# Moving a reload, reordering the engines' lists and letting TensorE add the residual of one feature tile in a graph-network kernel

## Chip, cores, metric

One NeuronCore of a Trainium2 chip (trn2). The metric is the device time in microseconds, the median of some runs; lower is better. The program has one launch and all data is in HBM at the start.

## What is computed

The input x has 1250 nodes with 512 features, and 20000 edges (src, dst) sorted by dst. Cut to what matters:

```
h    = relu(layernorm(x))                        # 1250 x 512
xn   = batchnorm(h) * g1 + b1
agg  = segment_sum(xn[src], dst) / max(deg, 1)
conv = relu(agg @ W_conv + b_conv)
attn = performer_attention(h[first 256 positions], Wq, Wk, Wv, proj) @ Wo
out  = x + batchnorm(conv + attn + h) * g2 + b2  # per feature, over the 1250 nodes
```

The attention has 8 heads of 64 and 256 random features; only 256 positions take part, and nodes behind them get the last one's result.

## The kernel before

The program is written out by hand, one list of instructions for each engine; semaphores join them. The eight PSUM banks go round in a fixed order (`order`, `order_end`); `pe_open` waits until the last user of a bank has been read, `landed(eng, name)` waits until TensorE has filled the bank of that name, `stored(eng, name)` until the bank has been read. `link` makes VectorE wait for its own last instruction.

**Front.** Ten node tiles of x are loaded into `xs`, normalised (VectorE statistics, ScalarE `ln_tile`), turned by TensorE and stored feature-major in `hT` by ScalarE (`store_hT`). In VectorE's list come then `edge_values` (the edge list's arithmetic), `weight_sizes` (L1100, waits for W_conv), `constants` (L1086 to L1095), `edge_columns` (L1105, L1106, then a wait until ScalarE has read the bank), the batchnorm statistics `bn_piece(0..2)` (L1040), `bn_mean`, `column_scales`, `bn_scale` and the first `one_hots` (L1054). ScalarE's `edge_columns` (L394, L395) waits for `flag_ready`, which VectorE gives at L1106. TensorE does the attention's projections, then `count()` (L621, a group of 10 one-hot products that counts edges), then `values(0, 0)` and `values(0, 1)` (L630).

**Middle.** 25 groups of edges go round: VectorE `one_hots`, TensorE `count`, ScalarE `store` (L387) into the adjacency `A16`; a count waits until the store two groups before is done. Between them stand the projection of the nodes, `project(i, half)` (L676), which reads `xnT`, made by ScalarE in three parts, `normal_xT(0..2)` (L457), and which ScalarE `high_part` (L497) and VectorE `low_part` (L1193) split into two f16 parts `gh`, `gl`; and the attention. `xnT` lies in the same memory as `xs`, so x must be loaded again for the last sum: SyncE's list has that reload (L306) behind `landed(sp, "G", 9)`, the last projection. `q_feat(7)` is ScalarE's (L479).

**Branch.** Behind the last `attn_T(1)` (L711) TensorE reads `flag` and branches over a block (`uncovered_edges`) that handles edge lists which the fast counting can't cover; with these inputs the block is skipped. Behind it stand `heads_out` (L719, 16 matmuls of 128x128 by 128x256 f32, each of them two records in the trace) and then the edge sums `aggregate(f, c)` (L936), for four feature tiles f and three chunks c of nodes.

**End.** For each feature tile VectorE makes y (`y(f, c)`, L1331, L1336) and its statistics (L1338), `moments` (L1342, L1344) and `scale` (six dependent small steps, L997 to L1000, L1350, L1351), with a square root by ScalarE (L581) between. ScalarE applies scale and shift (L584), TensorE turns the tile back (`transpose_z`, L954), VectorE adds x in place in `xs` (`finish`, L1361), and SyncE and ScalarE issue the stores (L334, L338, L588, L590). Ahead of the last feature tile's transposes stand `LATE` = 14 matmuls whose result nobody reads (L945).

Of the kernel before, what the change touches and what calls it, by code (L numbers as in the profile page):

```python
# [5 lines left out]
ALU = mybir.AluOpType  # L6
# [8 lines left out]
P = 128  # L15
# [27 lines left out]
LATE = 14  # L43
# [11 lines left out]
def gnn_kernel(nc, x, src, dst, g1, b1, g2, b2, w_conv, b_conv, w_q, w_k, w_v, w_o, proj, out):  # L55
    with ExitStack() as ctx:
# [168 lines left out]
        def read(*name):  # L225
            return bank_read[uses[name][0]]
# [77 lines left out]
        def _(sp):  # L304
# [22 lines left out]
            landed(sp, "G", NT - 1)  # L327
# [45 lines left out]
        def _(act):  # L373
# [17 lines left out]
            def edge_columns():  # L391
                acc = landed(act, "cols")
                act.wait_ge(flag_ready, 1)
                act.activation(bcol[:, :, :], acc[:, 0:NW].unsqueeze(2).to_broadcast([P, NW, 2]), ACT.Copy)  # L394
                act.activation(vcol[:, :, :], acc[:, NW:2 * NW].unsqueeze(2).to_broadcast([P, NW, 2]), ACT.Copy  # L395
                               ).then_inc(read("cols"), 1)
# [149 lines left out]
            normal_xT(2)  # L546
            k_exps(1, 1)
            store()
            q_feat(7)
# [3 lines left out]
            store()  # L553
            high_part(6)
            store()
# [9 lines left out]
            attn_copy(0)  # L565
            high_part(9)
# [9 lines left out]
            for c, (c0, cn) in enumerate(CHUNKS):  # L576
                acc = landed(act, "rdeg", c)
                act.activation(rdeg[:, c0:c0 + cn], acc[:, 0:cn], ACT.Copy).then_inc(read("rdeg", c), 1)  # L578
            for f in range(FT):
# [3 lines left out]
                for a, b in ((0, 512), (512, 1024), (1024, N)) if f < FT - 1 else ((0, 512), (1024, N)):  # L583
                    act.activation(yT[:, f, a:b], yT[:, f, a:b], ACT.Identity,  # L584
                                   bias=t2[:, f:f + 1], scale=s2[:, f:f + 1]).then_inc(z_act, 1)
# [8 lines left out]
        def _(pe):  # L594
# [239 lines left out]
            count()  # L834
            pe.wait_ge(wv_in, 16)
            values(0, 0)
            values(0, 1)
# [101 lines left out]

            def transpose_z(f):  # L940
                for j in range(3):
                    acc = pe_open(pe, "zT", f, j)
                    if (f, j) == (FT - 1, 0):
                        for k in range(LATE):
                            nc.tensor.matmul(acc[:, :], cone[:, :], A16[:, 0, 0:512], start=True, stop=True)  # L945
                    if f < FT - 1:
                        pe.wait_ge(z_act, 3 * f + j + 1)
                    elif j == 1:
                        pe.wait_ge(z_dve, 1)
                    else:  # L950
                        pe.wait_ge(z_act, 3 * f + j // 2 + 1)
                    for i in range(4 * j, min(4 * j + 4, NT)):
                        o = (i - 4 * j) * P
                        last = nc.tensor.transpose(acc[:, o:o + P], yT[:, f, i * P:(i + 1) * P], ident[:, :])  # L954
                    last.then_inc(full("zT", f, j), 1)
# [26 lines left out]
            transpose_z(FT - 2)  # L982
# [4 lines left out]
        def _(dve):  # L987
# [115 lines left out]
            def edge_columns():  # L1103
                acc = landed(dve, "cols")
                link(V.tensor_scalar(fl[0:1, 1:2], acc[0:1, 2 * NW:2 * NW + 1], float(NW * P - E), None, ALU.is_equal))  # L1105
                V.tensor_copy(flag[:, :], fl[0:1, 1:2]).then_inc(flag_ready, 1)  # L1106
                stored(dve, "cols")

# [122 lines left out]
            bn_scale()  # L1231
            one_hots()
# [44 lines left out]
            one_hots()  # L1277
            k_feat(1)
# [32 lines left out]
            def last_phase(slow):  # L1311
# [28 lines left out]
                def moments(f):  # L1340
                    c = slice(f, f + 1)
                    V.bn_aggr(mv2[:, f, :], st2[:, f, :, :].rearrange("p c s -> p (c s)")).then_inc(bn2_var, 1)  # L1342
                    dve.wait_ge(bn2_var, f + 1)
                    V.tensor_scalar(bw2[:, 3, c], mv2[:, f, 0:1], -1.0, None, ALU.mult)  # L1344

                def scale(f):
# [3 lines left out]
                    link(V.tensor_tensor(s2[:, c], bw2[:, 1, c], vec[:, 4 * V_G2 + f:4 * V_G2 + f + 1], ALU.mult))  # L1350
                    V.scalar_tensor_tensor(out=t2[:, c], in0=s2[:, c], scalar=bw2[:, 3, c],  # L1351
                                           in1=vec[:, 4 * V_B2 + f:4 * V_B2 + f + 1], op0=ALU.mult, op1=ALU.add).then_inc(st2_ready, 1)
# [25 lines left out]
                finish(f - 1, 0)  # L1378
# [4 lines left out]
                finish(f - 1, 1)  # L1383
                finish(f - 1, 2)
# [81 lines left out]
```

## Time and profile before

| | us |
|---|---|
| median of 3 runs | 198.77 (198.75 to 200.66) |
| the profiled execution | 199.06 |
| its span, first to last instruction | 197.1 |
| TensorE busy in the span | 172.4 (87%) |
| VectorE, ScalarE busy | 130.9 (66%), 89.4 (45%) |
| mean granted TensorE clock | 0.964 of full speed |

The profiled execution is 1.96 us longer than its span; that part lies outside of the instructions. A share of busy time is a mean over stages with different limits.

### The profile page before, as it was taken

To read this page: it belongs to the slowest core of one execution; us is meant where nothing else is said; L and a number is where in the kernel's file an instruction comes from. 1 tells how busy PE (TensorE), PEld (TensorE's weight loads), DVE (VectorE), ACT (ScalarE), POOL (GpSimd) and SP (SyncE) were. 2 spreads that over 40 slices of the span, in tenths; PEclk is the share of its full clock that TensorE was granted. 3 is DMA by queue.
4 is the path that set the end of the run, shared out by engine and by line. 5 is a ranking of instruction groups with operands and counts; after the bars stand their busy time and mean duration, and the time that the engine had idled before them with its cause. 6 is when DMAs were issued, how large, how long until landed. Compare 5 with 4: busy or idle time off the path is not lost.

```text
span 197.1 us, 2982 instructions
## 1 busy us (share of the span) xinstructions
PE 172.4 (87%) x1115; PEld 115.7 (59%) x1116; DVE 130.9 (66%) x311; ACT 89.4 (45%) x159; POOL 7.6 (4%) x22
## 2 busy tenths in 40 slices
PE   0589999799999999979999995089999999999980
PEld 0568797644476546536777674068549465474740
DVE  3678879997465766987737846920203989497591
ACT  3339946285961779994433316001725040404030
POOL 5180000000000000000000000000000000000000
PEclk9999999969999999999999999658999999999999
DMA  5988910000330000000000006900000004022027
GB/s 185 377 246 245 384 37 0 0 0 5 84 145 0 3 0 0 0 5 0 0 3 0 3 0 191 328 7 0 0 0 3 0 0 130 3 62 69 0 61 200
DMA packets 11883, 13.69 MB, mean 69 GB/s; under 512 B 1458, under 2 KB 6748, under 8 KB 11868
## 3 DMA queue, kind: packets, MB, share of 16 engines
q1 hardware_dynamic: 10476, 12.13, 18.9%
q10 hardware_dynamic: 1072, 1.10, 1.7%
q0 software_dynamic: 320, 0.26, 0.7%
q8 instruction: 10, 0.16, 0.3%
q14 instruction: 5, 0.04, 0.1%
HBM read 10.92 MB, written 2.56 MB: 68 GB/s over the span
## 4 chain that ended last, share of the span: by engine, by line
PE 60%; DVE 13%; DMA 9%; ACT 8%; issue 6%; SPq 2%; ACTq 0%; DVEq 0%
PE bank L936 21%; PE bank L676 13%; PE bank L719 5%; DMA xs<-in_x 5%; PE bank L630 4%; DMA wc<-in_L_gnn_W_conv 4%; PE bank L700 4%; PE bank L690 4%; PE bank L621 3%; DVE st L1040 3%; PE bank L653 2%; SPq L306 2%; ACT r L492 2%; PE bank L954 1%; ACT r L387 1%
## 5 line engine op out<-in xcount | busy, mean ns | idle before, releaser
L676 PE MATMUL bank<-wc,xs 128*128 128x512 f32 (+1 forms) x80 | 38.6, 609 | 0.1
L936 PE MATMUL bank<-r,gl 128*128 128x512 f16 (+1 forms) x120 | 38.2, 338 | 0.0
L936 PE MATMUL bank<-r,gh 128*128 128x512 f16 (+1 forms) x120 | 38.1, 339 | 0.0
L1054 DVE TENSOR_TENSOR ohb<-iota,bcol 128x1280 f16<-128x1280 f16 x25 | 20.5, 819 | 4.9 <-PE bank L621 4.8
L387 ACT ACTIVATE r<-bank 128x500 f16<-128x500 f32 x25 | 18.7, 767 | 5.1 <-PE bank L621 5.0
L676 PEld LDWEIGHTS bank<-wc,xs 128*128 128x128 f32 (+1 forms) x80 | 13.6, 187 | 10.8 <-issue 10.8
L936 PEld LDWEIGHTS bank<-r,gl 128*128 128x128 f16 x120 | 11.7, 97 | 9.2
L936 PEld LDWEIGHTS bank<-r,gh 128*128 128x128 f16 x120 | 11.6, 97 | 9.1
L609 PE MATMUL bank<-hT,r 128*128 128x256 f32 x64 | 16.2, 412 | 0.7 <-issue 0.7
L719 PE MATMUL bank<-qe,wvo 128*128 128x256 f32 x32 | 10.1, 491 | 7.1 <-issue 7.1
L1331 DVE SCALAR_TENSOR_TENSOR r<-bank,cinv,r 128x512 f32<-128x512 f32 (+1 forms) x12 | 7.8, 646 | 12.0 <-ACT r L578 6.8
L621 PEld LDWEIGHTS bank<-ohv,ohb 128*128 128x128 f16 x250 | 9.8, 98 | 9.9 <-issue 7.2
L609 PEld LDWEIGHTS bank<-hT,r 128*128 128x128 f32 x64 | 13.0, 208 | 3.1 <-ACT hT L378 1.1
L719 PEld LDWEIGHTS bank<-qe,wvo 128*128 128x128 f32 x32 | 8.1, 256 | 9.0 <-issue 7.3
L581 ACT ACTIVATE bw<-mv,epst 128x1 f32<-128x1 f32 x4 | 1.2, 295 | 25.4 <-DVE mv L1342 25.4
L621 PE MATMUL bank<-ohv,ohb 128*128 128x50 f16 x250 | 10.6, 186 | 2.3 <-DVE ohv L1054 1.3
L1193 DVE SCALAR_TENSOR_TENSOR gl<-bank,gh 128x512 f16<-128x512 f32 (+1 forms) x10 | 6.9, 690 | 7.9 <-ACT gh L497 7.9
L497 ACT ACTIVATE gh<-bank 128x512 f16<-128x512 f32 (+1 forms) x10 | 6.0, 600 | 12.1 <-PE bank L676 12.1
L1054 DVE TENSOR_TENSOR ohv<-iota,vcol 128x500 f16<-128x500 f16 x25 | 10.3, 412 | 0.0
L584 ACT ACTIVATE r<-r,t,s 128x512 f32<-128x512 f32 (+1 forms) x11 | 7.2, 717 | 5.4 <-DVE t L1351 5.4
L630 PE MATMUL bank<-wvo,hT 128*128 128x512 f32 x16 | 9.0, 706 | 0.0
L457 ACT ACTIVATE xs<-hT,t,s 128x384 f32<-128x384 f32 (+2 forms) x12 | 7.8, 734 | 2.6 <-DVE t L1130 2.6
(167 smaller groups left out, 264.9 us busy)
## 6 DMA issues: line engine op xcount, KB each, us to landing
xs<-in_x SPq DMA_DIRECT2D x15, 256.0 KB, 5.0
out<-xs SPq DMA_DIRECT2D x7, 256.0 KB
r<-in_L_gnn_Wq SPq DMA_DIRECT2D x1, 1024.0 KB, 8.3
r<-in_L_gnn_Wk SPq DMA_DIRECT2D x1, 1024.0 KB, 6.2
wc<-in_L_gnn_W_conv SPq DMA_DIRECT2D x1, 1024.0 KB, 8.5
wvo<-in_L_gnn_Wv SPq DMA_DIRECT2D x1, 1024.0 KB, 11.2
wvo<-in_L_gnn_Wo SPq DMA_DIRECT2D x1, 1024.0 KB, 5.2
xs<-in_x ACTq DMA_DIRECT2D x3, 256.0 KB, 4.1
```

The costliest lines, as they stand in the source:

```text
L387: act.activation(A16[:, :, p * GW * W:(p + 1) * GW * W].rearrange("p a (q d) -> p q a d", q=GW), bank[p % 2][:, 0:GW * NT * W].rearrange(" ...
L457: act.activation(xnT[:, f, a:b], hT[:, f, a:b], ACT.Identity, bias=t1[:, f:f + 1], scale=s1[:, f:f + 1]).then_inc(xn_ready, 1)
L609: last = nc.tensor.matmul(acc[:, t * NA:(t + 1) * NA], w[:, f, c:c + P], hT[:, f, 0:NA], start=(f == 0), stop=(f == FT - 1))
L621: last = nc.tensor.matmul(bank[p % 2][:, q * NT * W:(q + 1) * NT * W], ohb[:, s, :], ohv[:, s, :], start=True, stop=True)
L630: last = nc.tensor.matmul(acc[:, :], hT[:, f, t * P:(t + 1) * P], wvo[:, f, :], start=(f == 0), stop=(f == FT - 1))
L676: last = nc.tensor.matmul(acc[0:n, :], xnT[:, f, i * P:i * P + n], wc[:, f, :], start=(f == 0), stop=(f == FT - 1))
L690: last = nc.tensor.matmul(acc[:, j * (DH + 1):(j + 1) * (DH + 1)], kf[:, t, h, m * P:(m + 1) * P], v1[:, t, h, :], start=(t == 0), stop=(t ...
L700: last = nc.tensor.matmul(acc[:, j * (DH + 1):(j + 1) * (DH + 1)], qfT[:, m, h, t * P:(t + 1) * P], kv[:, m, h, :], start=(m == 0), stop=( ...
L719: last = nc.tensor.matmul(acc[:, t * NA:(t + 1) * NA], wvo[:, c, o:o + P], attnT[:, c, :], start=(c == 0), stop=(c == FT - 1))
L936: last = nc.tensor.matmul(acc[:, 0:cn], gg[0:n, s, f * P:(f + 1) * P], A16[0:n, s, c0:c0 + cn], start=(s == 0 and gg is gh), stop=(s == NT ...
L1054: last = V.tensor_tensor(oh[:, s0:s0 + n, :].rearrange("p s (m t) -> p s m t", t=2), iota16[:, 0:size].rearrange("p (m t) -> p m t", t=2). ...
L1331: V.scalar_tensor_tensor(out=yT[:, f, c0:c0 + cn], in0=sums, scalar=cinv[:, f:f + 1], in1=rdeg[:, c0:c0 + cn], op0=ALU.mult, op1=ALU.mult) ...
```

## The change

- SyncE's reload of x waits for the first edge sum (`landed(sp, "agg", 0, 0)`) in place of the last projection.
- ScalarE's `edge_columns` no longer waits for VectorE's flag; it copies the one number that VectorE needs (`fl`) itself. VectorE's part goes behind `bn_scale`, and `bn_piece(0)` goes ahead of `weight_sizes`.
- TensorE's first `count()` goes behind `values(0, 0)`.
- In ScalarE's list `normal_xT(2)` goes from ahead of `k_exps(1, 1)` to behind `high_part(5)` and its two stores, and one `store()` goes ahead of `high_part(9)`; `q_feat(7)` goes to VectorE.
- Feature tile 2 (the third) is turned by matmuls with the identity that add x's tile in PSUM (`turn_with_residual`); ScalarE copies two of its three banks to `xs`, VectorE one, in place of VectorE's three `finish`. The 14 unread matmuls go.
- `scale(f)` has four dependent steps, not six; one short step goes to `moments`.
- ScalarE normalises nodes 0 to 511 of the last tile in two halves, and TensorE waits for each.

```diff
-            landed(sp, "G", NT - 1)
+            landed(sp, "agg", 0, 0)
             for i in range(NT):
                 load_x(i)
...
             def edge_columns():
                 acc = landed(act, "cols")
-                act.wait_ge(flag_ready, 1)
                 act.activation(bcol[:, :, :], acc[:, 0:NW]...)
...
+                act.activation(fl[0:1, 1:2], acc[0:1, 2 * NW:2 * NW + 1], ACT.Copy).then_inc(read("cols"), 1)
...
+            k_exps(1, 1)
+            store()
+            high_part(5)
+            store()
+            store()
             normal_xT(2)
-            k_exps(1, 1)
-            store()
-            q_feat(7)
-            store()
-            high_part(5)
-            store()
-            store()
             high_part(6)
...
+            def copy_turned(f, j):
+                a, b = 4 * j, min(4 * j + 4, NT)
+                acc = landed(act, "zT", f, j)
+                act.activation(xs[:, a:b, f * P:(f + 1) * P], acc[:, 0:(b - a) * P]..., ACT.Copy).then_inc(read("zT", f, j), 1)
+
             for f in range(FT):
+                if f == FT - 1:
+                    copy_turned(f - 1, 0)
                 act.wait_ge(bn2_var, f + 1)
                 act.activation(bw2[:, 0, f:f + 1], mv2[:, f, 1:2], ACT.Sqrt, bias=epst[:, 0:1]).then_inc(bn2_std, 1)
+                if f == FT - 1:
+                    copy_turned(f - 1, 1)
                 act.wait_ge(st2_ready, f + 1)
-                for a, b in (...) if f < FT - 1 else ((0, 512), (1024, N)):
+                for a, b in (...) if f < FT - 1 else ((0, 256), (256, 512), (1024, N)):
...
             features("uk", kT, 1)
-            count()
             pe.wait_ge(wv_in, 16)
             values(0, 0)
+            count()
             values(0, 1)
...
+            def turn_with_residual(f):
+                for j in range(3):
+                    acc = pe_open(pe, "zT", f, j)
+                    pe.wait_ge(z_act, 3 * f + j + 1)
+                    tiles = range(4 * j, min(4 * j + 4, NT))
+                    for i in tiles:
+                        pe.wait_ge(x_in[i], 32)
+                    for i in tiles:
+                        n, o = rows_of(i), (i - 4 * j) * P
+                        nc.tensor.matmul(acc[:, o:o + P], yT[:, f, i * P:(i + 1) * P], ident[:, :], start=True, stop=False)
+                        last = nc.tensor.matmul(acc[0:n, o:o + P], ident[0:n, 0:n], xs[0:n, i, f * P:(f + 1) * P],
+                                                start=False, stop=True)
+                    last.then_inc(full("zT", f, j), 1)
...
-            transpose_z(FT - 2)
+            turn_with_residual(FT - 2)
             transpose_z(FT - 1)
...
             edge_values()
+            bn_piece(0)
             weight_sizes()
             constants()
-            edge_columns()
-            bn_piece(0)
             bn_piece(1)
             link(bn_piece(2))
             bn_mean()
             column_scales()
             bn_scale()
+            edge_columns()
             one_hots()
...
-                    rstd(mv2[:, f, 1:2], bw2[:, 0, c], bw2[:, 1, c], bw2[:, 2, c])
-                    link(V.tensor_tensor(s2[:, c], bw2[:, 1, c], vec[...], ALU.mult))
+                    link(V.reciprocal(bw2[:, 1, c], bw2[:, 0, c]))
+                    V.tensor_tensor(s2[:, c], bw2[:, 1, c], vec[...], ALU.mult)
+                    link(V.scalar_tensor_tensor(out=bw2[:, 0, c], in0=bw2[:, 1, c], scalar=bw2[:, 2, c], in1=bw2[:, 1, c], ...))
+                    link(V.scalar_tensor_tensor(out=s2[:, c], in0=bw2[:, 0, c], scalar=1.5, in1=s2[:, c], ...))
...
                 moments(f)
-                finish(f - 1, 0)
                 scale(f)
...
-                finish(f - 1, 1)
-                finish(f - 1, 2)
+                acc = landed(dve, "zT", f - 1, 2)
+                V.tensor_copy(xs[:, 8:NT, (f - 1) * P:f * P], ...)
```

## Rows read from the trace of the kernel before

Timeline rows are: start, length, engine, line, operation, out<-in, shape, count, and in brackets the idle time before with what ended it. SPq is SyncE's queue. In the rows of stretches (A:B) stand the stretch's length, then busy time of PE, PEld, DVE, ACT and POOL with counts, then the granted TensorE clock, the DMA engines' mean busy share and GB/s. "issue" is time in which an engine waited for nothing that the profile shows.

**Rows 1.** The page: granted clock in 40 slices; the instruction queue of section 3

```profile
PEclk9999999969999999999999999658999999999999
...
q8 instruction: 10, 0.16, 0.3%
```

**Rows 2.** The chain that ended last: start, length, what

```profile
46.44 1.80 PE bank L630 x4
...
121.94 0.61 ACT qe L467
122.54 6.49 issue
129.04 10.06 PE bank L719 x32
```

**Rows 3.** Timeline around the branch: SyncE's queue, the reload of x

```profile
118.60 4.68 SPq L306 DMA_DIRECT2D xs<-in_x  x10
```

**Rows 4.** Stretches around the branch, and one in the edge sums

```profile
121.90:124.60 2.70, 0.00 (x0) 0.00 (x0) 2.49 (x5) 0.60 (x1) 0.00 (x0) 1.00 0.92 296
124.60:127.90 3.30, 0.00 (x0) 0.00 (x0) 3.09 (x5) 0.00 (x0) 0.00 (x0) 0.52 0.94 346
127.90:129.00 1.10, 0.00 (x0) 0.00 (x0) 1.03 (x3) 0.00 (x0) 0.00 (x0) 0.50 0.06 22
...
129.00:134.80 5.80, 5.76 (x14) 4.63 (x15) 0.33 (x2) 0.00 (x0) 0.00 (x0) 0.50 0.01 3
...
148.90:149.30 0.40, 0.40 (x6) 0.40 (x6) 0.00 (x0) 0.38 (x1) 0.00 (x0) 1.00 0.19 41
```

**Rows 5.** Timeline of VectorE, front

```profile
23.58 2.50 DVE L1100 SCALAR_TENSOR_TENSOR gh<-wc 128x512 bf16<-128x512 f32 x4 [0.30 <-DMA wc<-in_L_gnn_W_conv]
...
28.93 6.02 DVE L1040 BATCH_NORM_STATS2 st<-hT 128x6 f32<-128x512 f32 x12 [1.20 <-ACT vcol L395]
...
38.28 0.82 DVE L1054 TENSOR_TENSOR ohb<-iota,bcol 128x1280 f16<-128x1280 f16 x1
```

**Rows 6.** Timeline of ScalarE, front

```profile
21.91 1.06 ACT L378 ACTIVATE hT<-bank 128x512 f32<-128x512 f32 x2
...
27.83 0.59 ACT L394 ACTIVATE bcol<-bank 128x500 f16<-128x500 f32 x1 [2.75 <-DVE flag L1106]
...
29.95 1.94 ACT L378 ACTIVATE hT<-bank 128x512 f32<-128x512 f32 x4
```

**Rows 7.** Timeline of TensorE, front

```profile
39.49 0.60 PE L621 MATMUL bank<-ohv,ohb 128*128 128x50 f16 x10 [1.28 <-DVE ohv L1054]
...
44.94 1.13 PE L653 MATMUL bank<-pT,qT 64*128 64x256 f32 x8
```

**Rows 8.** A stretch of the front, TensorE's clock in it

```profile
39.40:42.60 3.20, 3.11 (x13) 1.58 (x14) 3.17 (x7) 3.17 (x7) 0.00 (x0) 0.50 0.00 0
```

**Rows 9.** Timeline of the middle: waits of VectorE and TensorE, ScalarE's third part of xnT

```profile
61.32 0.17 DVE L1135 COPY diag<-bank 128x16 f32<-128x16 f32 x1 [2.23 <-PE bank L644]
...
83.22 2.40 ACT L457 ACTIVATE xs<-hT,t,s 128x354 f32<-128x354 f32 x4
...
88.01 0.41 PE L621 MATMUL bank<-ohv,ohb 128*128 128x50 f16 x10 [1.07 <-ACT r L387]
```

**Rows 10.** Timeline of VectorE: the first sums with the reloaded x

```profile
163.03 1.60 DVE L1361 TENSOR_TENSOR xs<-bank,xs 128x512 f32<-128x512 f32 x3
```

**Rows 11.** Groups by line and shape, 100 to 197 us: 10 matmuls f32

```profile
L971 PE MATMUL bank<-ident,dcol 128*128 128x128 f32 x20 | 2.4, 275 | 0.0
```

**Rows 12.** Timeline of the end, all engines

```profile
187.02 3.19 PE L945 MATMUL bank<-r,cone 128*128 128x512 f16 x14
...
188.10 0.68 DVE L1361 TENSOR_TENSOR xs<-bank,xs 128x512 f32<-128x512 f32 x1
...
189.92 1.28 ACT L584 ACTIVATE r<-r,t,s 128x512 f32<-128x512 f32 x2 [1.59 <-DVE t L1351]
...
192.54 0.38 SPq L334 DMA_DIRECT2D out<-xs  x1
```

More of the change, by code:

```diff
@@ L42 @@
 SLOW_LINKS = 8
-LATE = 14
 EP, EJ = 125, E // 125
@@ L545, in _ @@
             store()
-            normal_xT(2)
             k_exps(1, 1)
-            store()
-            q_feat(7)
             store()
@@ L553, in _ @@
             store()
+            normal_xT(2)
             high_part(6)
+            store()
             store()
@@ L578, in _ @@
                 act.activation(rdeg[:, c0:c0 + cn], acc[:, 0:cn], ACT.Copy).then_inc(read("rdeg", c), 1)
+            def copy_turned(f, j):
+                a, b = 4 * j, min(4 * j + 4, NT)
+                acc = landed(act, "zT", f, j)
+                act.activation(xs[:, a:b, f * P:(f + 1) * P], acc[:, 0:(b - a) * P].rearrange("p (t n) -> p t n", t=b - a),
+                               ACT.Copy).then_inc(read("zT", f, j), 1)
             for f in range(FT):
+                if f == FT - 1:
+                    copy_turned(f - 1, 0)
                 act.wait_ge(bn2_var, f + 1)
                 act.activation(bw2[:, 0, f:f + 1], mv2[:, f, 1:2], ACT.Sqrt, bias=epst[:, 0:1]).then_inc(bn2_std, 1)
+                if f == FT - 1:
+                    copy_turned(f - 1, 1)
                 act.wait_ge(st2_ready, f + 1)
-                for a, b in ((0, 512), (512, 1024), (1024, N)) if f < FT - 1 else ((0, 512), (1024, N)):
+                for a, b in ((0, 512), (512, 1024), (1024, N)) if f < FT - 1 else ((0, 256), (256, 512), (1024, N)):
                     act.activation(yT[:, f, a:b], yT[:, f, a:b], ACT.Identity,
@@ L949, in transpose_z @@
                         pe.wait_ge(z_dve, 1)
-                    else:
-                        pe.wait_ge(z_act, 3 * f + j // 2 + 1)
+                    elif j == 2:
+                        pe.wait_ge(z_act, 3 * f + 3)
                     for i in range(4 * j, min(4 * j + 4, NT)):
+                        if f == FT - 1 and i in (0, 2):
+                            pe.wait_ge(z_act, 3 * f + i // 2 + 1)
                         o = (i - 4 * j) * P
@@ L1277, in _ @@
             one_hots()
+            q_feat(7)
             k_feat(1)
@@ L1344, in moments @@
                     V.tensor_scalar(bw2[:, 3, c], mv2[:, f, 0:1], -1.0, None, ALU.mult)
+                    V.tensor_scalar(bw2[:, 2, c], mv2[:, f, 1:2], EPS, -0.5, ALU.add, ALU.mult)
                 def scale(f):
@@ L1348, in scale @@
                     dve.wait_ge(bn2_std, f + 1)
-                    rstd(mv2[:, f, 1:2], bw2[:, 0, c], bw2[:, 1, c], bw2[:, 2, c])
-                    link(V.tensor_tensor(s2[:, c], bw2[:, 1, c], vec[:, 4 * V_G2 + f:4 * V_G2 + f + 1], ALU.mult))
+                    link(V.reciprocal(bw2[:, 1, c], bw2[:, 0, c]))
+                    V.tensor_tensor(s2[:, c], bw2[:, 1, c], vec[:, 4 * V_G2 + f:4 * V_G2 + f + 1], ALU.mult)
+                    link(V.scalar_tensor_tensor(out=bw2[:, 0, c], in0=bw2[:, 1, c], scalar=bw2[:, 2, c], in1=bw2[:, 1, c],
+                                                op0=ALU.mult, op1=ALU.mult))
+                    link(V.scalar_tensor_tensor(out=s2[:, c], in0=bw2[:, 0, c], scalar=1.5, in1=s2[:, c],
+                                                op0=ALU.add, op1=ALU.mult))
                     V.scalar_tensor_tensor(out=t2[:, c], in0=s2[:, c], scalar=bw2[:, 3, c],
```

12 lines of the change are left out of this document (4 added, 8 removed).

## The prediction

> **What bounds the kernel now.** I read the granted clock and the queue table of the page first, then the chain that ended last, then the timelines of the engines around each edited step. TensorE is busy for 172.4 of 197.1 us, so the time is its work plus its holes plus what a halved clock costs. The page shows the clock below full at two places, in slice 9 and slices 26 to 28 of 40 [rows 1]; both lie at edits. The large one: the last product ahead of the branch is turned and copied by 122.54, then nothing happens on the chain for 6.49 us, and only at 129.04 does `heads_out` start and take 10.06 us [rows 2]. The reload of x is issued from 118.60 on in ten DMAs [rows 3]; the DMA engines are 92 and 94% busy until 127.90, then one sixteenth of them works for 1.1 us at 22 GB/s (24 KB, a page of instructions of 16 KB and a remainder, or so I read it; the instruction queue moved 10 packets in 0.16 MB, 16 KB each [rows 1]), and then TensorE goes on [rows 4]. My reading: the taken branch needs instructions that must come by DMA, and they come behind x. The clock falls in this hole and stays at 1.2 GHz (0.50) to 134.8, 5.8 us of work [rows 4].
>
> The small one: TensorE waits 1.28 us for the first one-hots, then works 3.1 us at 0.50 [rows 7, 8]. A third hole of 1.07 us lies at 88.01, ended by a store of ScalarE [rows 9]. At the end, the chain leaves TensorE: statistics, scale, normalise, turn, add, store.
>
> **Front, part by part.** VectorE now has 0.30 us of waiting for W_conv and 1.20 us for ScalarE's reading of the columns [rows 5]. `bn_piece(0)` needs node tiles 0 to 3, stored by 22.97 [rows 6], so it starts at 23.3 with no wait. Four 512-column statistics, at 6.02 us for eight of 512 and four of 226 columns, are 2.5 us: to 25.8. `weight_sizes` 2.5 us to 28.3, `constants` 1.4 us to 29.7. ScalarE no longer stands for 2.75 us at the flag [rows 6]; its two column copies and the small one fall into that wait, and its tile stores, which began at 29.95, begin some 0.7 us earlier, when TensorE's key product permits. So tiles 6 and 7 are stored by 30.2, `bn_piece(1)` runs to 32.7, `bn_piece(2)` to 33.9, where before statistics ended at 34.95 [rows 5]. The moved flag step costs 0.2 us ahead of the one-hots. Net about 1.0 us: the one-hots begin at 37.4 and not 38.28, and end at 38.5.
>
> TensorE itself was free at 39.49 - 1.28 = 38.21 [rows 7]. With `values(0, 0)` first it needs no one-hots then: 1.80 us (two matmuls at full clock, the first row of [rows 2]) to 40.0, the count 0.25 us, `values(0, 1)` 1.80 us, so 42.05 against 44.94: 2.9 us, if the clock holds. If the clock falls at 39.3 and rises at 42.6 as now [rows 8], 1.1 us of work is done before, 1.65 in the slow stretch, and the remaining 1.1 ends at 43.7: 1.25 us. I take 2.9, since the hole is gone and dense 512-column work stands in it, bounds 1.2 and 2.9. VectorE and ScalarE are only 1.0 ahead there, yet VectorE stands 2.23 us for TensorE's diagonal at 61.32 [rows 9], and ScalarE then waits for VectorE, so they catch up.
>
> **Middle.** The wait of 1.07 us at 88.01 is for ScalarE's store behind `normal_xT(2)` and `k_exps(1, 1)` [rows 9]. With the 2.3 us of `normal_xT(2)` moved behind, that store comes 2.2 us earlier: the hole closes, 1.05 us. Followed on in before's times, `normal_xT(2)` then runs from 88.8 to 91.0, and `project(7, 0)`, its first reader, comes at 95.0; `q_feat(7)` on VectorE costs it 0.6 us in the 0.9 us in which it waited for ScalarE's exponentials, and the key features are ready at 88.1 for 89.0. Those covers are 4 us and 0.9 us wide; if the second were gone, it would cost up to 0.6. The store ahead of `high_part(9)` fits in a pause of ScalarE: nothing.
>
> **Branch.** The reload now starts after the first edge sum, so nothing but the fetch is in the DMA queues at the branch. No row shows a fetch alone from the branch on. Bounds: `heads_out` can't start before 122.54 [rows 2], a gain of 6.5; and if the queue was not the cause, 0. Nearest row: the 1.1 us of transfer behind the reload [rows 4]. With the branch at about 121.5 and as long again for its way as for its transfer, 2.2 to 2.5 us, TensorE starts at 124.0. Gain 5.0. **Clock:** the fall came 2.7 us after TensorE stood still, at 124.6 [rows 4]; 2.1 us is a shorter hole, but 1.28 us was enough in the front. I expect it to fall and to rise sooner, since dense work then follows at once: 3.3 us slow as in the front [rows 8] and not 5.8, so 1.65 lost in place of 2.9. Gain 1.25, bounds 0 and 2.9.
>
> The Trainium skill (Runtime: NRT & Kernel Launch, section "Instruction fetch mechanics") says that a taken branch out of the fetched pages forces a fetch by DMA, with which the row agrees; but it gives TensorE a buffer of 2048 instructions. By that figure the target would be there already, and the start would be 122.6, the first rival below; no row here shows the buffer's size.
>
> **Reload at its new place.** It starts when the first edge sum ends and takes 9.3 us as now (118.60 to 127.90). Its reader is the sum of tile 0, at 163.03 in before's times [rows 10]: with the first edge sum's end at 143.4, over 10 us of room. SyncE's stores stand behind it in the queue, and are due later still. It meets TensorE's next page of instructions, at 148.9 now [rows 4], about 139 then.
>
> **End.** TensorE turns and adds tile 2 in 20 f32 matmuls; ten of that shape took 2.4 us [rows 11], so 4.5 to 4.8, begun at 185.9 and finished at 190.5; the transposes and the unread matmuls in their place end at 190.2 [rows 12]. So 0.3 us more, and the clock is held by it. VectorE sheds 0.68 us ahead of its scale [rows 12] and two dependent steps, 0.38, but gets 0.15 in `moments`, and ScalarE's first copy (0.6, of one bank as the copy at 121.94 in [rows 2]) runs when the square root is due, so about 0.4 is left: 189.5 and not 189.88 for the shift. ScalarE's second copy waits for a bank that is full at 189.5, and takes 0.6 ahead of the normalisation, which so starts at 190.1, not 189.92: the gain is spent. The half-size first piece gives 0.3 back. VectorE has three adds less, so SyncE's queue is free earlier: the store of the last tile's first bank, held to 192.54 by it [rows 12], goes at about 192.1. The last DMA's landing then sets the end. I take 0.3, bounds -0.3 (the copy) and 0.9.
>
> **Sum.** 2.9 + 1.05 + 5.0 + 1.25 + 0.3 = 10.5 on the profiled 199.06: 188.6. The median is 0.3 below the profiled execution: 188.3, say 188.4.
>
> **Rivals.**
> *The target's instructions are there already.* The hole shrinks to 0.6 us of attention copy, the clock perhaps never falls: 1.4 more from the start and up to 1.65 more from the clock: 185.4 to 187.0. For: the skipped block is short, some 200 matmuls with their weight loads. Against: 7.1 us of standing still with nothing else to wait for. 0.15.
>
> *The hole isn't the queue's doing.* A branch that costs 7 us by itself, or something else that the profile calls issue. The front and middle gains stay: 198.8 - 2.9 - 1.05 - 0.3 = 194.5. For: no row shows a branch without the reload. Against: TensorE resumes 1.1 us after the transfers end. 0.12. The Trainium skill speaks for this rival (DMA: Bandwidth & Descriptors, "Queues, rings and completion order"): each DMA engine goes round between the queues it has work for, a packet at a time. Then the page would not have waited behind all of x.
>
> *The clock falls in the front all the same*, or VectorE's lead of only 1.0 us is what counts: 1.2 in place of 2.9, 190.1. 0.20.
>
> *The stall only moves, and the kernel gets slower.* The reload now lies on the edge sums, and a page of instructions is due there. Should TensorE stand until the transfers end, it loses up to 9.3 us, and 2.9 by the clock, 12.2 in all against the sum of 10.5: 200.5. It decides from the point at which the page is needed before the reload ends. Against: pages come some 20 us apart there and 148.9 is the fetch, not the need, with TensorE at work all through. 0.04.
>
> *The end goes wrong* (ScalarE's copies, SyncE): within the range.
>
> **How the numbers follow.** Forecast 0.49 at 188.4, with its own bounds 186.5 to 190; the others 0.15 at 186, 0.12 at 194.5, 0.20 at 190.1, 0.04 at 200.5. A range of 185.8 to 192.0 leaves out the last and the hole that stays, and a little of the first: below 0.2. About 1% is what a measurement of this kernel can tell from no change: 196.8 and 200.8. Below 196.8 lie all but the moved stall and odd mixtures: 0.94 faster, 0.03 within, 0.03 slower.
>
> **What would show it.** After: no hole at the first count and the clock at 1.00 around 40; no wait at the count behind `project(5, 1)`; the SyncE rows of the reload behind the first edge sum; "issue" ahead of L719 of 1.5 to 3 us with few GB/s in it; L719 at 8.5 to 9 us; no hole in L936. Wrong would be: a hole before L719 as wide as now, a hole in the edge sums, or ScalarE and VectorE as the chain between 45 and 88, where they have less lead than TensorE.

## The result and the profile after

| | before | after |
|---|---|---|
| median, us | 199.06 (198.75 to 200.66, 4 runs) | 194.19 (193.36 to 194.64, 4 runs) |
| ratio, 95% interval | | 0.9735 (0.9672 to 0.9798) |
| profiled execution, its span | 199.06, 197.1 | 194.64, 192.2 |

The kernel is faster by 4.9 us where 10.4 were forecast, and the time lies above the range. (Before's median is of one run more than at the start, hence 199.06 and not 198.77.) Medians here and below are over all runs of a kernel, ratios and their intervals over its fast runs alone, those within 1.5% of its fastest. The two spans differ by 4.9 us as well, so the two traces can be laid side by side. First the chain that ended last in the kernel after, around the branch (start, length, what):

```profile
120.58 0.64 PE bank L719 x4
121.22 0.02 issue
121.25 0.60 ACT qe L465
121.85 3.52 issue
125.38 8.74 PE bank L727 x32
```

These answer to [rows 2]: the hole behind ScalarE's attention copy (L465) is 3.52 and not 6.49 us, and `heads_out` (L727 now) takes 8.74 and not 10.06. Stretches of the same place, and of the reload at its new place (columns as in [rows 4]):

```profile
121.20:121.70 0.50, 0.01 (x1) 0.00 (x0) 0.47 (x2) 0.45 (x1) 0.00 (x0) 1.00 0.00 0
121.70:122.20 0.50, 0.00 (x0) 0.00 (x0) 0.50 (x1) 0.15 (x1) 0.00 (x0) 0.58 0.00 0
122.20:122.70 0.50, 0.00 (x0) 0.00 (x0) 0.47 (x2) 0.00 (x0) 0.00 (x0) 0.50 0.16 33
122.70:123.20 0.50, 0.00 (x0) 0.00 (x0) 0.47 (x2) 0.00 (x0) 0.00 (x0) 0.50 0.00 0
...
124.70:125.20 0.50, 0.00 (x0) 0.00 (x0) 0.47 (x2) 0.00 (x0) 0.00 (x0) 0.50 0.00 0
...
140.00:142.00 2.00, 2.00 (x11) 0.89 (x10) 0.00 (x0) 0.00 (x0) 0.00 (x0) 1.00 0.95 298
...
144.00:146.00 2.00, 2.00 (x22) 1.99 (x21) 0.11 (x1) 1.69 (x4) 0.00 (x0) 1.00 1.00 362
```

The DMA engines are empty in the hole but for one burst of 33 GB/s in 0.5 us. That is 16 KB, the size of one packet of the instruction queue. It has passed by 122.7, yet TensorE starts only at 125.38. The clock fell at about 121.8, 0.6 us after TensorE's last work, and rose at about 128.5; in before it fell only 2.7 us after [rows 4]. The reload, from 138.5 on, fills the DMA engines for some 9 us and TensorE has no gap in it.

The front is where the forecast and the trace part most. VectorE and TensorE of the kernel before, waits in brackets, at the point where the gathered edge rows arrive and at the key projection behind it:

```profile
19.43 0.30 DVE L1068 TENSOR_SCALAR r<-r 125x256 int32<-125x256 int32 x1 [0.40 <-DMA r<-in_dst,rows]
...
24.30 3.72 PE L609 MATMUL bank<-hT,r 128*128 128x256 f32 x16
```

VectorE of the kernel after:

```profile
21.46 0.29 DVE L1089 TENSOR_SCALAR r<-r 125x256 int32<-125x256 int32 x1 [3.51 <-DMA r<-in_dst,rows]
...
25.49 2.47 DVE L1061 BATCH_NORM_STATS2 st<-hT 128x6 f32<-128x512 f32 x4 [0.19 <-issue]
...
33.91 3.65 DVE L1061 BATCH_NORM_STATS2 st<-hT 128x6 f32<-128x512 f32 x8 [2.13 <-ACT hT L377]
...
40.97 0.80 DVE L1075 TENSOR_TENSOR ohb<-iota,bcol 128x1280 f16<-128x1280 f16 x1
```

TensorE of the kernel after, and a stretch of it with the granted clock:

```profile
25.36 0.65 PE L785 MATMUL bank<-ident,r 125*128 125x125 f32 x4 [1.93 <-DVE r L1102]
25.93 0.24 PE L787 MATMUL bank<-ones,nout 125*1 125x1 f32 x4
26.10 5.41 PE L617 MATMUL bank<-hT,r 128*128 128x256 f32 x16
...
41.51 1.98 PE L638 MATMUL bank<-wvo,hT 128*128 128x512 f32 x4
...
45.48 1.13 PE L661 MATMUL bank<-pT,qT 64*128 64x256 f32 x8
...
26.20:28.20 2.00, 2.00 (x5) 1.63 (x6) 2.00 (x4) 1.09 (x3) 0.00 (x0) 0.50 0.04 8
```

The wait of 1.28 us at the first count [rows 7] is gone, as forecast: `values(0, 0)` starts at 41.51 with no idle time. But VectorE's edge arithmetic waited 3.51 us for the gathered edge rows, which came at 21.46; in the profile before they had come at 19.43. TensorE then idles 1.93 us before it can turn the edge columns (L785), the clock falls there (0.50 in the stretch), and the next product (L617, the key projection's first half) takes 5.41 us where it took 3.72. The features of q start at 45.48, against 44.94 [rows 7].

So the 4.9 us of the two spans split like this:

| stretch, us | before | after | gain | forecast |
|---|---|---|---|---|
| start to the features of q | 44.94 | 45.48 | -0.5 | 2.9 |
| from there to the last copy ahead of `heads_out` | 77.0 | 75.8 | 1.2 | 1.05 |
| from that copy's start to `heads_out` | 7.1 | 4.1 | 3.0 | 5.0 |
| `heads_out` | 10.06 | 8.74 | 1.3 | 1.25 |
| from there to the span's end | 58.0 | 58.1 | -0.1 | 0.3 |

### The profile page after: what moved, and what is told of

Same layout as the page of the kernel before. It is cut to its first block, busy times and chain, and to the rows that moved or that the text cites. A ratio compares the mean times of both kernels' runs of the same rounds, so it can differ in the third digit from the quotient of the medians.

```text
span 192.2 us, 3020 instructions
## 1 busy us (share of the span) xinstructions
PE 171.7 (89%) x1131; PEld 117.3 (61%) x1132; DVE 129.5 (67%) x309; ACT 90.0 (47%) x162; POOL 7.5 (4%) x22
## 3 DMA queue, kind: packets, MB, share of 16 engines
q1 hardware_dynamic: 10476, 12.13, 19.4%
## 4 chain that ended last, share of the span: by engine, by line
PE 77%; issue 7%; DVE 4%; DMA 4%; ACT 3%; POOL 2%; POOLq 1%; DVEq 0%; ACTq 0%
PE bank L944 22%; PE bank L684 17%; PE bank L617 5%; PE bank L727 5%; PE bank L638 4%; DMA r<-in_dst,rows 4%; PE bank L708 4%; PE bank L698 4%; PE bank L661 3%; PE bank L629 3%; PE bank L672 2%; PE bank L652 2%; PE bank L975 2%; POOL r L365 1%; PE bank L992 1%
## 5 line engine op out<-in xcount | busy, mean ns | idle before, releaser
L1075 DVE TENSOR_TENSOR ohb<-iota,bcol 128x1280 f16<-128x1280 f16 x25 | 20.4, 817 | 4.2 <-PE bank L629 4.1
L684 PEld LDWEIGHTS bank<-wc,xs 128*128 128x128 f32 (+1 forms) x80 | 13.6, 187 | 10.9 <-issue 10.9
L617 PE MATMUL bank<-hT,r 128*128 128x256 f32 x64 | 18.0, 447 | 0.7 <-issue 0.7
L617 PEld LDWEIGHTS bank<-hT,r 128*128 128x128 f32 x64 | 14.3, 228 | 3.7 <-ACT hT L377 1.1
L727 PE MATMUL bank<-qe,wvo 128*128 128x256 f32 x32 | 8.7, 441 | 4.2 <-issue 4.2
L727 PEld LDWEIGHTS bank<-qe,wvo 128*128 128x128 f32 x32 | 7.2, 227 | 5.6 <-issue 4.4
L629 PE MATMUL bank<-ohv,ohb 128*128 128x50 f16 x250 | 10.4, 184 | 0.0
L587 ACT ACTIVATE bw<-mv,epst 128x1 f32<-128x1 f32 x4 | 1.2, 292 | 19.4 <-DVE mv L1362 19.4
L592 ACT ACTIVATE r<-r,t,s 128x512 f32<-128x512 f32 (+2 forms) x12 | 7.5, 689 | 3.0 <-DVE t L1376 3.0
L397 ACT ACTIVATE xs<-xs,lnw 128x512 f32<-128x512 f32 x10 | 7.4, 802 | 2.1 <-DVE lnw L1054 2.1
```

What stands on the lines that cost most here:

```text
L617: last = nc.tensor.matmul(acc[:, t * NA:(t + 1) * NA], w[:, f, c:c + P], hT[:, f, 0:NA], start=(f == 0), stop=(f == FT - 1))
L629: last = nc.tensor.matmul(bank[p % 2][:, q * NT * W:(q + 1) * NT * W], ohb[:, s, :], ohv[:, s, :], start=True, stop=True)
L684: last = nc.tensor.matmul(acc[0:n, :], xnT[:, f, i * P:i * P + n], wc[:, f, :], start=(f == 0), stop=(f == FT - 1))
L727: last = nc.tensor.matmul(acc[:, t * NA:(t + 1) * NA], wvo[:, c, o:o + P], attnT[:, c, :], start=(c == 0), stop=(c == FT - 1))
L1075: last = V.tensor_tensor(oh[:, s0:s0 + n, :].rearrange("p s (m t) -> p s m t", t=2), iota16[:, 0:size].rearrange("p (m t) -> p m t", t=2). ...
```

## The experiments

Before was measured again beside each set of experiments: 199.16 us (e1 to e4), 199.0 (e5 to e8), 199.57 (e9 to e12) and 199.06 (e13, e14). Single runs of it lay between 195.1 and 201.1, so a difference of less than 1 us between two of the medians says little. A kept trace shows where time went, but it is one execution, and not always a typical one. "After" is the changed kernel.

**The reload: e1, e4.** e1 is after with the old wait, e4 is before with the new one.

```diff
-            landed(sp, "agg", 0, 0)
+            landed(sp, "G", NT - 1)
```

> The changed kernel with the reload of x behind the last projection again, all else as changed. Theory (the branch's fetch of instructions takes about 4 us by itself, and waits behind the reload when that fills the DMA queues): TensorE idle ahead of heads_out goes from 4.2 us to 7 us, heads_out from 8.7 to about 10 us, span 192.2 to about 196.5; ratio to before about 0.99. Rival (the hole shrank for another reason, such as the order of the last stores): TensorE idle stays at 4.2 us and the span within 0.7 us of 192.

Measured: 195.53 (195.01 to 199.19), ratio 0.9863 (0.9758 to 0.9969). Its chain has the hole and the slow `heads_out` back:

```profile
121.84 6.01 issue
127.86 9.59 PE bank L727 x32
```

3.35 us more than after's in the two rows, and 195.5 against 192.2 in the span, where the rest is the same: as the theory had it, a little less than the 4.3 expected. But the traced execution, 197.32, is not typical: it is the longest but one of e1's five, and three of the others have spans of 192.8 to 193.4, against 191.3 to 192.2 in after's four. By the medians, which were not measured together, the old place costs 1.3 us, by the ratios (0.9863 against 0.9735) 2.5.

> The kernel before with the reload moved alone. Theory: idle ahead of heads_out 4.2 us and not 7.1, heads_out about 8.7 us, so 3 + 1.3 = 4.3 us off the span of 197.1: 192.8, ratio 0.978. Rival (the move gains only with the other edits): ratio 0.99 or more. Its front is that of before: a second look at when the gathered edges land (19.4 in the first trace of before, 21.4 in that of after).

Measured: 196.93, ratio 0.9921 (0.9875 to 0.9968). Nine of its ten runs took 195.53 to 198.06 and one 355.05, which nothing here explains. In the profile:

```profile
124.41 3.62 issue
128.03 9.91 PE bank L719 x32
```

and two stretches of the hole:

```profile
126.50:126.80 0.30, 0.00 (x0) 0.00 (x0) 0.30 (x1) 0.00 (x0) 0.00 (x0) 0.99 0.00 0
126.80:127.00 0.20, 0.00 (x0) 0.00 (x0) 0.20 (x1) 0.00 (x0) 0.00 (x0) 0.50 0.00 0
```

The hole shrinks as in after, by 2.9 us. But `heads_out` gained 0.15 us and not 1.3: here the clock fell only at 126.8, 3 us after TensorE stopped and 1.2 before it went on, and stayed down for more than 5 us of its work, where after had 3.2. Also the gathered rows came at 21.61, so that the span of 196.0 is only 1.1 below before's. The shorter hole is seen in every profile with the reload moved; what the clock gives back differs from run to run. By its ratio, a gain of 1.6 us (0.6 to 2.5), e4 sits with the rival; by its rows with the theory.

**The branch: e2, e3, e10.** e2 and e3 leave out TensorE's read of the flag, its branch and with it the rare edge lists; e3 has the reload back besides.

```diff
             attn_T(1)
-            uncovered_edges()
```

> The changed kernel without TensorE's read of the flag and its branch; it leaves out TensorE's handling of edge lists that the fast counting can't cover. Theory (what is left of the hole is the branch's own fetch): TensorE idle ahead of heads_out falls from 4.2 us to 0.65 us, the attention copy; heads_out runs at full clock in 7.2 us; span 192.2 - 3.5 - 1.5 = 187. Rival (something else holds heads_out, such as the load of Wo or a bank): idle stays above 3 us.

> No branch of TensorE (as in the run before) and the reload behind the last projection again. Theory (the reload hurts only through the branch's fetch): idle ahead of heads_out 0.65 us as without the reload there, span within 0.7 us of the run without branch, about 187. Rival (the reload holds TensorE in another way, by SBUF or by semaphores): idle 3 us or more, span 190 or more.

Measured: e2 190.48 (187.95 to 191.57), span 186.1; e3 188.83 (187.81 to 191.01), span 187.4. TensorE of e2 at the place, by timeline (start, length, and the idle time ahead in brackets):

```profile
121.18 7.14 PE L727 MATMUL bank<-qe,wvo 128*128 128x256 f32 x32 [0.89 <-ACT qe L465]
```

and the same instructions of e3:

```profile
122.21 7.14 PE L727 MATMUL bank<-qe,wvo 128*128 128x256 f32 x32 [0.92 <-ACT qe L465]
```

Without a branch `heads_out` waits for the attention copy alone, and takes 7.14 us at full clock in both. (The traces are of runs with a mean clock of 0.997 and 0.996; runs of the same kernels at 0.976 to 0.988 took 189.93 to 191.57 us.) In e3 ten DMAs of x are issued from 117.99 to 122.6 and fill the engines (374 GB/s from 122.2 to 126.0), and TensorE doesn't feel them. So the wait behind the attention copy is 0.25 us with neither (e2), 0.28 with the reload alone (e3), 3.5 with the branch alone (after), and 6.0 with both (e1). The reload hurts only through the branch. The span of e3 is 1.3 us longer than that of e2, where up to 0.7 was expected: its gathered rows came at 22.72 against 21.72, and q's features start 1.0 us later.

e10 keeps the branch and turns it round:

```diff
-                with pe.If(covered == 0):
-                    ... (the rare block)
-            ... (heads_out and all behind it)
+            at = opened[0]
+            with pe.If(covered == 1):
+                rest()                 # heads_out and all behind it
+            with pe.Else():
+                opened[0] = at
+                uncovered_edges()      # the rare block
+                rest()
```

> The changed kernel with TensorE's branch turned round: the block for normal inputs, with all that follows, stands directly behind the branch, and the rare block with a second copy of what follows stands in the else. Theory (only a taken branch has to fetch): idle ahead of heads_out 0.65 us and not 4.2, clock at full, heads_out 7.2 us, as without the branch: 3.5 + 1.6 = 5 us below the changed kernel, 189. Rival (reading the flag, or any branch, stops the fetch): idle 3 us or more, 194. A jump over the else comes then at TensorE's end, where it has 4 us.

Measured: 189.45 (188.7 to 190.17), ratio 0.9583 (0.9514 to 0.9651). TensorE of e10 by timeline:

```profile
121.45 7.14 PE L727 MATMUL bank<-qe,wvo 128*128 128x256 f32 x32 [0.88 <-ACT qe L465]
```

and a stretch of e10 with the flag's reading in it:

```profile
120.20:121.00 0.80, 0.37 (x4) 0.13 (x2) 0.77 (x1) 0.40 (x1) 0.00 (x0) 1.00 0.00 0
```

From 118.0 to 128.0 the DMA engines move nothing, there is no hole but the copy's, and the clock stays at full. Reading the flag costs nothing that shows; it is the taken branch. The median is 4.4 us below that of e9, the kernel with the old branch that was measured beside it, and 4.6 below e5's. Unlike e2, e10 still handles the rare edge lists; TensorE's program holds all that follows twice.

**The front: e5, e6, e13, e8, e14.** e5 is after and e13 is before, both unaltered. e6 is after with the front's edits undone:

```diff
             edge_values()
-            bn_piece(0)
             weight_sizes()
             constants()
+            edge_columns()             # with ScalarE's wait for the flag
+            bn_piece(0)
             bn_piece(1)
...
-            values(0, 0)
             count()
+            values(0, 0)
```

> The changed kernel once more, unaltered, for pairing with the others of this call and as a second look at its front. Theory (the gathered edge rows land at 21.4 us or later whenever the load of Wk is issued ahead of the last gather's landing, and the first trace of before, with 19.4, was the exception): they land at 21 us or later again. Rival (the changed lists delay the gather, or it is chance of half and half): 19.5 us, and then features of q start at about 42.5 us and not 45.5. Span 191 to 192.5.

> The changed kernel with the front's edits undone (VectorE's order, ScalarE's wait for the flag, the count ahead of values). Theory (the front edits gain 1.3 to 2.3 us when the gather lands late, since a hole of 1.3 us and a slow clock at the first count come back): q's features start at 46.8 us, 1.3 to 2.3 us later than with the edits; time 1.5 to 2.3 us above that of the changed kernel. Rival (my prediction's size): 2.9 us. Rival (nothing gained in the front): within 0.5 us.

> The kernel before, unaltered, for a second profile of its front. Theory (the first profile of before caught the gathered rows early, at 19.4 us; in eleven of the other profiles they landed at 19.9 to 22.7): they land at 20.5 us or later, by the time of Wk's issue, and the features of q start at 46 us or later and not at 44.9. Rival (it is a property of before's lists): 19.4 us and 44.9 us again.

Measured: e5 194.02 (193.06 to 195.36); e6 195.15 (194.04 to 197.77), 1.1 us above it, a little less than expected; e13 198.86, its one run. What their fronts show, beside the others':

| profile | rows land at | clock in the front | features of q | from landing |
|---|---|---|---|---|
| before | 19.43 | falls at the first count | 44.94 | 25.5 |
| e4, before's front | 21.61 | falls at the first count | 46.82 | 25.2 |
| e13, before's front | 21.57 | holds | 45.10 | 23.5 |
| e6, before's front | 21.75 | falls ahead of L618 | 46.18 | 24.4 |
| after | 21.46 | falls ahead of L617 | 45.48 | 24.0 |
| e5, after's front | 20.55 | falls ahead of L617 | 44.57 | 24.0 |
| e2, after's front | 21.72 | holds | 44.58 | 22.9 |
| e10, after's front | 21.99 | holds | 44.85 | 22.9 |

The four other profiles with after's front fit in: e1, e7 and e9, where the clock fell, need 24.0, 23.9 and 24.0 us from the landing, and e3, where it held, 22.8. In e5 the rows came somewhat earlier than expected.

TensorE of e13:

```profile
41.22 0.43 PE L621 MATMUL bank<-ohv,ohb 128*128 128x50 f16 x10 [1.23 <-DVE ohv L1054]
41.49 3.68 PE L630 MATMUL bank<-wvo,hT 128*128 128x512 f32 x8
45.10 1.14 PE L653 MATMUL bank<-pT,qT 64*128 64x256 f32 x8
```

The hole is there, 1.23 us, and the clock did not fall in it; the rows came late, at 21.57, and yet q's features started at 45.10 and not at 46 or later as I had written for late rows, since the clock held. So two things differ from run to run in the front, and my one profile showed neither: when the rows come, and whether the clock falls. Like against like, the front's edits are worth 0.4 us (the clock falls at the key projection in both: e6 24.4, after 24.0), 0.6 us (it holds: 23.5 to 22.9) or 1.2 us (it falls in both, in e4 at the first count: 25.2 to 24.0); 1.1 by the medians.

Why the rows come late: e8 and e14 make SyncE wait for them ahead of the weights, e8 ahead of all but Wk, e14 ahead of Wk too.

```diff
             sp.wait_ge(x_in[NT - 1], 16)
+            (e14: for i in range(4): sp.wait_ge(g_in[i], 16))
             sp.dma_start(wk, ...)
+            (e8:  for i in range(4): sp.wait_ge(g_in[i], 16))
             sp.dma_start(wc[:, :, :], ...)
             sp.dma_start(wvo[:, :, :], ...)
```

> The changed kernel with SyncE waiting for the gathered edge rows before it issues the loads of W_conv and Wv (Wk stays ahead). Theory (the rows land late because 3 MB of weights are ahead of them in the DMA queues): they land at about 18 to 19 us, TensorE's hole of 1.9 us at 23.4 closes, W_conv lands at about 27 us; time 1 to 2 us below the changed kernel. Rival (W_conv's later landing costs what the rows give): no difference, VectorE waits for W_conv.

> The changed kernel with all three weight loads issued behind the landing of the gathered rows. Theory (the weights ahead of them in the queues delay them): the rows land at 17.5 us or earlier, against 20.0 to 20.4 with Wk alone ahead and 21.4 to 22.7 with all three; Wk lands at about 24 and TensorE's key projection waits little, W_conv about 27; time within 1 us of e8 (192.9). Rival (the gather needs this long by itself): 20 us or later.

Measured: e8 192.93 (191.47 to 193.62), ratio 0.9666 (0.9618 to 0.9714); e14 192.27 (191.24 to 192.75), ratio 0.9788 (0.9651 to 0.9925), measured at another time than e8, and with a ratio that rests on two of before's seven runs. e8 is 1.1 us below e5. The rows were in at 20.2 in e8, with Wk alone ahead, and not at 18 to 19 as expected; TensorE's hole ahead of the columns closed. SyncE's queue in e14, where the issue itself marks the landing:

```profile
17.62 0.37 SPq L321 DMA_DIRECT2D r<-in_L_gnn_Wk  x1
```

They land at 17.6 us with nothing ahead, at 19.9 to 20.4 with 1 MB (e8, e11, e12), at 20.6 to 22.7 with 3 MB and after's front: the weights ahead in the queues delay them. W_conv's later landing cost nothing that shows. With the rows at 17.6 another wait takes over: in e14 VectorE waits 1.95 us for ScalarE's tiles ahead of `bn_piece(0)`, which starts at 24.51 and in e8 at 24.27. So e14 gains nothing on e8 there: q's features start at 43.38 in e14 and at 43.10 in e8.

**The end: e7, e9, e12.** e7 is after with the end of before.

```diff
-            turn_with_residual(FT - 2)
+            transpose_z(FT - 2)        # with the 14 unread matmuls, VectorE's three sums, six steps
```

> The changed kernel with the end undone: transposes and unread matmuls in place of the matmuls that add x, VectorE's three sums, six steps for the scale, one piece for nodes 0 to 511. Theory: from the end of the last edge sum to the end of the span 11.2 us with either; time within 0.4 us of the changed kernel. Rival (the new end is a gain hidden by another loss): 0.5 us or more slower.

Measured: 192.84 (192.43 to 195.55), ratio 0.9668 (0.9627 to 0.9709): 1.2 us below e5's median, which was not expected. Five of its eight runs took 192.4 to 192.9 and three 194.3 to 195.6; the trace kept is of one at 194.3, so it can't show what made the five shorter. The profiles don't show a gain. From the end of edge sum (3, 1) VectorE's last sum starts after 8.53 us in before and 8.52 in e7, but after 8.86 in after; the span ends after 12.94, 12.99 and 13.02. ScalarE of the kernel after, by timeline, shows why its last sums are late:

```profile
184.73 0.60 ACT L580 ACTIVATE xs<-bank 128x512 f32<-128x512 f32 x1 [1.01 <-PE bank L958]
185.22 1.55 ACT L592 ACTIVATE r<-r,t,s 128x256 f32<-128x256 f32 x3
```

and VectorE of the same kernel, whose sums wait for it:

```profile
186.83 1.62 DVE L1386 TENSOR_TENSOR xs<-bank,xs 128x512 f32<-128x512 f32 x3 [0.79 <-PE bank L975]
```

Scale and shift are ready at 184.70, 5.5 us behind the end of edge sum (3, 1), where before took 5.7. But ScalarE, waiting for a bank since 183.7, then copies it first and normalises from 185.22. e9 gives that copy to VectorE:

```diff
-                if f == FT - 1:
-                    copy_turned(f - 1, 1)                       # ScalarE
+                acc = landed(dve, "zT", f - 1, 1)               # VectorE, behind its normalisation
+                V.tensor_copy(xs[:, 4:8, ...], acc...).then_inc(read("zT", f - 1, 1), 1)
```

> The changed kernel with the second bank's copy of feature tile 2 by VectorE, behind its own piece of the normalisation, and not by ScalarE ahead of its piece. Theory (ScalarE's copy holds its normalisation for 0.5 us and with it the last transposes): VectorE's last sums start 0.5 us earlier against the end of the last edge sum (5.4 and not 5.9 us behind), the end from there 10.4 to 10.9 and not 11.1 us; time 0.2 to 0.6 us below the changed kernel. Rival (the last stores are bound by the DMA queues): no difference.

Measured: 193.89 (192.88 to 194.63), ratio 0.9794 (0.9719 to 0.9869). VectorE's last sum comes after 8.37 us, 0.5 earlier as expected; the span ends after 12.66 us and not 13.02, and the median doesn't tell it from after's (the two were not measured together).

**Together: e11, e12.** e11 has e10's branch, e9's copy and e8's loads; e12 has e10's branch and e8's loads, with the old end.

> The branch turned round, the second copy on VectorE and the loads of W_conv and Wv behind the gathered rows, together. Theory: 5 + 1 + 0.4 us below the changed kernel, 187.5 to 188.5, ratio 0.945. Rival: the parts hide each other, 189 or more.

> The branch turned round and the loads behind the gathered rows, with the end of the kernel before (transposes, unread matmuls, VectorE's sums, six steps). Theory (the new end is worth nothing, by the spans; the 1.2 us by which the run with the end undone was faster were other places' luck): within 0.5 us of e11. Rival (the new end costs about 1 us, in the last store's issue and behind the span): 1 us faster than e11.

Measured: e11 188.09 (186.73 to 189.13), ratio 0.9492 (0.9403 to 0.958); e12 188.45 (186.56 to 189.03), ratio 0.9493 (0.9405 to 0.9582). Equal: the new end is worth nothing, and e7's 1.2 us was not seen a second time. e11 and e12 are the fastest kernels found, 11 us below before. In both profiles the clock fell all the same as `heads_out` started, behind an idle time of 0.89 us, and `heads_out` took 8.83 us; in e10, behind 0.88 us, the clock held and it took 7.14:

```profile
120.00:121.00 1.00, 1.00 (x4) 0.80 (x5) 0.93 (x3) 0.00 (x0) 0.00 (x0) 0.69 0.00 0
```

This is e11's stretch from the start of its `heads_out`, with TensorE busy throughout and a mean granted clock of 0.69; in the same way e12 shows 0.56 from 120.0 to 121.0, and e10 1.00 over all of its `heads_out`. It is a matter of the run and not of the kernel: by the mean granted clock of each run, e11's six runs fall in two groups: three of 186.7 to 187.2 us at 0.996 or 0.997, three of 189.0 to 189.1 at 0.985 or 0.986. e12 has two of the first kind and four of the second, e10 four (0.995, 0.996) and two (0.985, 0.987). So 1.7 us are to be had or lost there by the run, and the traces of e11 and e12 are of the second kind.

## Why the prediction was wrong

**Right: the mechanism at the branch, its cause and its place.** The stall was that of a taken branch behind the reload; after, e1, e2 and e3 take the two apart, and e10 shows that it is the taking. **Wrong: its size.** The step that failed is "with the branch at about 121.5 and as long again for its way as for its transfer, 2.2 to 2.5 us, TensorE starts at 124.0". The branch costs 4.2 us of standing still by itself, 3.5 behind the copy: gain 3.0 in place of 5.0. I had doubled the transfer of 1.1 us; the burst is seen to pass in half a microsecond, and TensorE starts 2.7 us after it. The cost lies in what comes after the transfer, so the row of the transfer was the wrong one to take it from. (If the 2.7 us hold with the reload too, the awaited page passed before 126.4, among x's packets, and the 22 GB/s behind them [rows 4] were another transfer; that is worked out, not seen.) What TensorE waits for in these 2.7 us no view shows. Over several runs the reload's move is worth less still: 1.3 to 2.5 us by e1 against after, 1.6 by the ratio of e4, where the sum had 5.0 + 1.25 for hole and clock.

**Right in the pair, less as a mean: the clock at `heads_out`.** It gave 1.3 us in the pair, and the loss left, 8.74 against 7.14 at full clock, is the 1.6 us of the forecast. Over the profiles it is less: `heads_out` takes 10.06, 9.59 and 9.70 us with the reload at its old place, 8.5 to 9.4 in seven of eight profiles with it moved, and 9.91 in e4; the means are 0.8 us apart.

**Wrong: the front, 2.9 us.** The step was "TensorE itself was free at 38.21; with `values(0, 0)` first ... 42.05 against 44.94, if the clock holds". The first part is right, the hole closed. But of the 5.45 us between the first count and q's features 1.6 were a fall of the clock that happens in one execution and not in the next (3.88 us in e13, with the same hole), and in after it fell at another hole. And I took the arrival of the gathered rows, 19.4 us, as fixed; it was the earliest of all profiles with the loads in their places. With the rows at 21.4 and the clock down at the key projection, TensorE's work from the columns on is itself the chain, and the edits that give VectorE and ScalarE time find no one waiting: VectorE now waits 2.13 us for ScalarE's tiles (0.44 in e2 and e10, where the clock held). The front is worth 0.4 to 1.2 us. My own rival for it, 1.2 and 190.1 in total, had the right size.

**Right: the middle**, where the wait of 1.07 us [rows 9] is gone in every profile with the edit, and is 1.07 again in e4 and e13, which lack it. No kernel isolates it, and where the rest of the pair's 1.2 comes from isn't shown. **Nearly right: the end**, 0.3 forecast and nothing found; the point about ScalarE's second copy, that it spends the gain, was the right one, as e9 shows.

**The rivals.** "Already there" fell: a fetch is seen and waited for. "Not the queue's doing" fell as it stood, since the hole does shrink in e4 and in every profile with the reload moved; but 4.2 of the 7.1 us are the branch's own cost, so it was more than half right, and its 194.5 lies next to the result. "The stall only moves" fell: TensorE is busy 2.00 of 2.00 us under the reload.

**The range.** It took in the bounds of the branch up to a gain of 0 only in a rival of 0.12, and no case with branch and front both small. With 3.0 and 1.1 in the sum it gives 6.7 us, 192.1. What makes up the 2.1 us that are left to 194.2 stays open, and two things have that size. Between the two traces it is the front: 1.6 us less than 1.1, because after's trace has the rows 2.0 us later. But before with late rows (e13, 198.86) took no longer than before with early ones (199.06), as its clock held, so this doesn't carry over to the medians. Over several runs it may as well be the reload's move, 1.3 to 2.5 us in place of the 4.3 that the pair of traces shows.

**What was read of fetches and queues.** Without the taken branch there is neither the burst nor the 3.5 us of hole (e10 against after). The Trainium skill (Runtime: NRT & Kernel Launch, section "Instruction fetch mechanics") says that a taken branch out of the fetched pages forces a fetch, and these traces agree. The buffer of 2048 instructions that it states for TensorE did not spare TensorE the stall for a target some 400 instructions on (an estimate from the skipped block's 190 matmuls, each with its weight load). With the reload in the queues the hole was 2.5 to 3.0 us longer; at the branch, at 121.9, the reload had 6 us to go. The Trainium skill (DMA: Bandwidth & Descriptors, section "Queues, rings and completion order") says that each DMA engine takes turns between its queues by packets, and a fetch that waits for a part of the reload fits that; it does not make the fetch free.

## What to carry to other kernels

Put the usual case directly behind a branch, so that it isn't taken; a taken branch cost TensorE 4.2 us here with idle queues and 7.1 behind a full one. Before a gain is read from one trace, ask of each start in it whether it is the program's or the run's: the arrival of a DMA that races with others, and whether the clock fell in a short hole, moved the front by 2 and 1.6 us. Then ask the medians too: the trace of e1 gives the reload's move 3.35 us, the times 1.3 to 2.5. Issue small DMAs that a chain waits for ahead of large ones that have time, and let them land first.

## What was new of the hardware

- A taken branch of TensorE with idle DMA queues: 16 KB in a burst between 122.2 and 122.7, TensorE at work at 125.38, 4.2 us after its last work (3.9 to 4.3 in the seven other profiles with it). The branch turned round and not taken: no burst and 0.88 us, 0.61 of it the attention copy.
- The clock fell to 1.2 GHz in or right behind holes of 1.28 us (before), 1.22 (e4) and 0.89 us (e11, e12), and held at 2.4 GHz in holes of 1.23 us (e13), 1.07 us [rows 9] and 0.88 us (e10). The same hole of one program, before's at the first count, fell on either side. So did the one ahead of the turned columns in after's front: the clock fell in a hole of 1.39 us (e5) and held in one of 1.53 (e3).
- In the hole of 4 us at the branch the clock fell 0.6 us after TensorE stopped in after and 3 us after in e4; `heads_out` took 8.74 and 9.91 us.
- Gathers of 4 times 64 KB by GpSimd with 3 MB of weights queued about them landed between 19.4 and 22.7 us, with 1 MB at 19.9 to 20.4, with none at 17.6.

Open: why e7's median was 1.2 us below e5's; how long the holes are in the runs whose traces weren't kept; and why the spans of e10, e11 and e12 end 13.2 to 13.6 us behind edge sum (3, 1) and the others' 12.7 to 13.0. TensorE's own jump over the else at its end may be it; no run takes it apart.
